# The end of self-attention in a fused transformer layer: first chunk normalized and scored earlier, last products in another order, later chunks ranked one feed-forward step later

## The reference

```python
def reference(x, ctx, mask, Wq, Wk, Wv, Wo, wq, wk, wv, wo, w_router, W1, b1, W2, b2):
    x = x + cross_attention(layernorm(x), ctx, mask)          # ctx: (32, 512, 384)
    x = x + causal_self_attention_with_rope(layernorm(x))     # Wo included in both
    h = layernorm(x)
    scores = h @ w_router                                     # (32, 64)
    top_scores, top_idx = top_k(scores, 32)                   # per sequence, half the tokens
    y = gelu(h[top_idx] @ W1 + b1) @ W2 + b2                  # 512 -> 2048 -> 512
    return x + h.at[top_idx].add(sigmoid(top_scores) * y)
```

## Time and profile before

| | us |
|---|---|
| median of 3 runs | 1379.94 (1377.67 to 1382.29) |
| the profiled execution's own time | 1377.36 |
| its span, first to last instruction | 1374.9 |
| TensorE busy in the span | 1341.6 |
| cross-attention ends, self-attention begins, about | 900 |
| step 14's last TensorE work ends, pe_end begins | 1133.7 |
| the feed-forward begins (first hidden) | 1170.9 |

### The profile page before, as it was taken

How to read it: one execution, slowest core, us unless ns; L and a number is a source line. 1 busy time by engine, 2 the same in 40 slices (tenths; PEclk the granted TensorE clock), 3 DMA queues, 4 the chain that set the end, 5 groups by cost and what they waited for, 6 DMA issues and landing times.

```text
span 1374.9 us, 33152 instructions
## 1 busy us (share of the span) xinstructions
PE 1341.6 (98%) x12984; PEld 1059.8 (77%) x12984; DVE 666.7 (48%) x1688; ACT 730.2 (53%) x1410; POOL 544.3 (40%) x284
## 2 busy tenths in 40 slices
PE   7999999999999999999999999999999998999998
PEld 6877777777777777777777777677888886878686
DVE  4254554554544544544544544455666567732323
ACT  6455655656656656656656656653333345453231
POOL 6442422422522422422432434724444444466342
PEclk9999999999999999999999999999999999999999
DMA  7021111011011010110120112010000002122241
GB/s 254 26 59 34 34 50 32 28 54 32 25 57 32 25 57 26 31 57 25 32 57 25 32 56 93 14 55 2 1 0 0 0 0 93 62 92 92 77 138 61
DMA packets 39324, 66.06 MB, mean 48 GB/s; under 512 B 4208, under 2 KB 8560, under 8 KB 39280
## 3 DMA queue, kind: packets, MB, share of 16 engines
q1 hardware_dynamic: 38848, 64.67, 14.7%
q10 hardware_dynamic: 432, 0.79, 0.2%
HBM read 61.25 MB, written 4.19 MB: 48 GB/s over the span
## 4 chain that ended last, share of the span: by engine, by line
PE 89%; DVE 2%; ACT 2%; issue 1%; POOL 1%; POOLq 0%; DVEq 0%; ACTq 0%
PE psum L204 39%; PE psum L957 9%; PE psum L252 8%; PE psum L1791 6%; PE psum L1762 6%; PE psum L222 5%; PE psum L240 5%; PE psum L261 3%; PE psum L972 3%; PE psum L990 1%; PE psum L1448 1%; PE psum L982 1%; PE psum L1000 1%; PE psum L1773 1%; PE psum L1019 0%
## 5 line engine op out<-in xcount | busy, mean ns | idle before, releaser
L300 ACT ACTIVATE PT<-psum 128x512 f32<-128x512 f32 x256 | 153.2, 598 | 228.4 <-PE psum L252 228.4
L287 ACT ACTIVATE prob<-prob,nmx 128x512 f32<-128x512 f32 x256 | 182.6, 714 | 94.4 <-DVE nmx L342 94.4
L356 DVE COPY V<-psum 128x512 f32<-128x512 f32 x128 | 88.5, 692 | 229.4 <-PE psum L204 229.4
L342 DVE CUSTOM_DVE_ANT_0 prob<-psum,mbias 128x512 f32<-128x512 f32 x256 | 165.4, 684 | 67.1 <-PE psum L222 67.1
L293 ACT ACTIVATE prob<-prob,rinv 128x512 f32<-128x512 f32 x256 | 182.7, 714 | 0.0
L489 POOL TENSOR_SCALAR ctx_a<-ctx_r 128x1536 fp32r<-128x1536 f32 x16 | 65.4, 4090 | 265.3 <-PE psum L204 265.1
L489 POOL TENSOR_SCALAR ctx_b<-ctx_r 128x1536 fp32r<-128x1536 f32 x16 | 65.4, 4090 | 252.3 <-PE psum L204 235.4
L252 PEld LDWEIGHTS psum<-ident,prob 128*128 128x128 f32 x1024 | 127.5, 141 | 34.4 <-issue 1.3
L252 PE MATMUL psum<-ident,prob 128*128 128x128 f32 x1024 | 153.2, 272 | 0.5 <-ACT PT L300 0.4
L204 PE MATMUL psum<-wv_h,ctx_b 128*128 128x512 f32 x384 | 144.4, 417 | 0.0
L204 PE MATMUL psum<-wv_h,ctx_a 128*128 128x512 f32 x384 | 142.2, 412 | 1.2 <-DVE K L356 1.2
(11 more groups left out here) (215 smaller groups left out, 2814.2 us busy)
## 6 DMA issues: line engine op xcount, KB each, us to landing
ctx_r<-in_ctx SPq DMA_DIRECT2D x32, 768.0 KB, 4.6
w_r<-in_L_ffn_W SPq DMA_DIRECT2D x64, 256.0 KB, 2.8
xres<-in_x SPq DMA_DIRECT2D x16, 256.0 KB, 2.6
out<-tok SPq DMA_DIRECT2D x13, 256.0 KB, 3.6
tok<-in_x SPq DMA_DIRECT2D x3, 1024.0 KB, 12.4
mask<-in_mask_BxS_bf SPq DMA_DIRECT2D x32, 64.0 KB, 4.1
tok<-in_x SPq DMA_DIRECT2D x4, 256.0 KB, 3.3
wq_r<-in_L_xattn_Wq SPq DMA_DIRECT2D x4, 256.0 KB, 5.0
```

What stands on the lines that cost most here:

```text
L287: act.activation(prob[:, r, :], prob[:, r, :], ACT.Exp, bias=nmx[:, r:r + 1], scale=-1.0, accum_out=rsum[:, r:r + 1]).then_inc(s_ex, 1)
L300: act.activation(PT[:, r, :, :].rearrange("p k n -> p (k n)"), T_bank, ACT.Copy).then_inc(s_Pt, 1)
L342: dve.tensor_tensor_reduce(prob[:, r, :], S_bank[r], mbias[:, b, :], 1.0, 3.0e38, ALU.add, ALU.min, nmx[:, r:r + 1]).then_inc(s_mx, 1)
L356: dve.tensor_copy(item_place(q, m), KV_bank[m % 2]).then_inc(s_KVe, 1)
```

## The change

No product is added or left out. Parts:

1. **Chunk 0 early.** The deviations of tiles 0 to 7 are made in step 13, those of tiles 8 to 11 in step 14 and dve_end, those of 12 to 15 at the end; before, tiles 0 to 11 in step 14. The four normalizations of chunk 0 move to the end of step 13 (one) and to the start of step 14 (three); chunk 0 takes slot 3 of xn4 and chunk 3 slot 0. Its four dots and the diagonal run in step 14 on VectorE; the statistics of tiles 12 and 13 move from step 14 and the last part of dve_end to its middle. Steps 12 and 13 are written out instead of being turns of the loop.
2. **The last products in another order** (pe_end). V of tile 15 comes after the last transposes of q and k, then the scores of tile 15, the spread of chunk 0, the output projection of tile 13, and only then probabilities and values of tile 14, its output projection (in bank 6), those of tile 15, the spread of chunk 1, both gathers of chunk 0, its transposes, the gathers of chunk 1, the last output projection (in bank 4). VectorE and ScalarE follow that order.
3. **Chunks 2 and 3 later.** The spread of chunk 2 moves from feed-forward step 0 to 1, its gathers from 1 to 2, the spread of chunk 3 behind the second product of step 2; the dots of chunk 2 on VectorE come behind the hid_l of step 0 instead of before the feed-forward. GpSimd's first w_l waits for the one-hots of chunk 1.

```diff
@@ pe3
-            if has(t + 1):
+            if has(t + 1) and not (isinstance(t, int) and t == G - 2):
                 at_least(pe, s3_od, t)
                 project(pe, bank[1], x3_h[:, nxt, :, :], x3_l[:, nxt, :, :], vw_h, vw_l).then_inc(s3_V, 1)
@@ act3
+            if isinstance(t, int) and t == G - 2:
+                act_normalize(act, 0, range(1, CH))
...
-            if isinstance(t, int) and t == G - 2:
-                act_deviations(act, MOST)
+            if isinstance(t, int) and t >= G - 3:
+                act_deviations(act, FIRST if t == G - 3 else MIDDLE)
                 act.activation(warm[:], epsb[:], ACT.Exp)
-                act.wait_ge(s3_K, G)
-                act.wait_ge(s4_nm, 1)
-                act_normalize(act, 0)
...
+            if isinstance(t, int) and t == G - 3:
+                act.wait_ge(s3_wd, 1)
+                act.wait_ge(s4_nm, 1)
+                act_normalize(act, 0, range(1))
@@ last_stats, new: like next_stats, but writes mv3 directly
+        def last_stats(dve, t):
+            dve.wait_ge(s3_x, t + 1)
+            dve.wait_ge(s4_mv, t)
+            dve.bn_stats(st1[:], tok[:, t, :]).then_inc(s4_st, 1)
+            dve.wait_ge(s4_st, t + 1)
+            dve.bn_aggr(mv3[:, t, :], st1[:]).then_inc(s4_mv, 1)
-        MOST, REST = slice(0, G - CH), slice(G - CH, G)
+        FIRST, MIDDLE, REST = slice(0, 2 * CH), slice(2 * CH, 3 * CH), slice(3 * CH, G)
@@ dve3
             if has(t + 1):
+                if isinstance(t, int) and t == G - 2:
+                    dve.wait_ge(s4_c, 16 * 7)
+                    for n in range(CH - 1):
+                        dve_dot(dve, n)
                 dve.wait_ge(s3_K, t + 2)
...
-            if isinstance(t, int) and t == G - 2:
-                dve_deviations(dve, MOST, 0)
...
             if has(t - 1):
                 dve_o(dve, t - 1, 1 - par)
+            if isinstance(t, int) and t == G - 3:
+                dve_deviations(dve, FIRST, 0)
...
-            if has(t - 2):
+            if isinstance(t, int) and t == G - 2:
+                dve_dot(dve, CH - 1)
+                dve_diagonal(dve, 0)
+            elif has(t - 2):
                 next_stats(dve, t - 2)
@@ steps
-            with eng.Fori(1, G // 2 - 1) as h:
+            with eng.Fori(1, G // 2 - 2) as h:
-            for t in range(G - 2, end):
+            for t in range(G - 4, end):
@@
-        BANKS_OF = [(3, 0, 1, 3), (3, 5, 6, 7), (2, 3, 2, 3), (2, 3, 2, 3)]
+        BANKS_OF = [(3, 0, 1, 3), (7, 2, 6, 7), (2, 3, 2, 3), (2, 3, 2, 3)]
@@ pe_end, after the transposes of q and k
+            project(pe, bank[1], x3_h[:, PAR, :, :], x3_l[:, PAR, :, :], vw_h, vw_l).then_inc(s3_V, 1)
+            pe.wait_ge(s3_qa, G)
+            pe.wait_ge(s3_kT, G)
+            pe.wait_ge(s3_ms, LAST)
+            scores(pe).then_inc(s3_S, 1)
+            pe_spread(pe, 0)
+            pe.wait_ge(s3_x, LAST - 2)
+            output_projection(pe, PAR).then_inc(s3_Wo, 1)
             pe.wait_ge(s3_pn, LAST)
-            pe.wait_ge(s3_qa, G)
             pe.wait_ge(s3_v, G)
             for h in range(2):
                 probabilities(pe, 1 - PAR, h).then_inc(s3_PT, 1)
-            pe.wait_ge(s3_kT, G)
-            pe.wait_ge(s3_ms, LAST)
-            scores(pe).then_inc(s3_S, 1)
             pe.wait_ge(s3_pa, 2 * LAST)
             values(pe, 1 - PAR).then_inc(s3_PV, 1)
-            pe.wait_ge(s3_x, LAST - 2)
-            output_projection(pe, PAR).then_inc(s3_Wo, 1)
-            pe.wait_ge(s3_x, LAST - 1)
+            pe.wait_ge(s3_ms, G)
             pe.wait_ge(s3_od, LAST)
-            output_projection(pe, 1 - PAR).then_inc(s3_Wo, 1)
-            pe_spread(pe, 0)
+            output_projection(pe, 1 - PAR, bank[6]).then_inc(s3_Wo, 1)
...
             values(pe, PAR, LAST_BANK).then_inc(s3_PV, 1)
+            pe_spread(pe, 1)
             pe_gather(pe, 0, 0)
             pe_gather(pe, 0, 1)
-            pe_spread(pe, 1)
+            pe_transpose(pe, 0)
             pe.wait_ge(s3_x, LAST)
-            pe.wait_ge(s3_od, G)
-            output_projection(pe, PAR).then_inc(s3_Wo, 1)
             pe_gather(pe, 1, 0)
             pe_gather(pe, 1, 1)
-            pe_transpose(pe, 0)
+            pe.wait_ge(s3_od, G)
+            output_projection(pe, PAR, bank[LAST_BANK]).then_inc(s3_Wo, 1)
             pe_transpose(pe, 1)
@@ act_end: q_T, k_T, v, normalize chunk 1, pT of 14, exp of 15, o_h of 14, three w_h,
@@ then half of chunk 2, pT of 15, o_h of 15, the other half of chunk 2, xs_h ...
@@ dve_end
+            dve_deviations(dve, MIDDLE, 1)
...          (mask and row maximum of tile 15)
+            dve_compare(dve, 0)
+            dve_dot(dve, CH)
+            dve_dot(dve, CH + 1)
+            add(LAST - 2, bank[2])
             dve_o(dve, LAST - 1, 1 - PAR)
...          (row sum and reciprocal of tile 15)
+            last_stats(dve, LAST - 3)
+            last_stats(dve, LAST - 2)
+            dve_dot(dve, CH + 2)
+            dve_dot(dve, CH + 3)
+            dve_diagonal(dve, 1)
             dve_one_hot(dve, 0)
+            add(LAST - 1, bank[6])
             dve_compare(dve, 1)
             dve_one_hot(dve, 1)
+            dve_o(dve, LAST, PAR, LAST_BANK)
@@ gpsimd, feed-forward
+                    if isinstance(n, int) and n == 0:
+                        pool.wait_ge(s4_oh, 2 * CH)
                     if isinstance(n, int) and n == 1:
-                        pool.wait_ge(s4_s, 2 * CH)
                         pool.wait_ge(s3_PV, G)
@@ vector, feed-forward
-                between = {0: lambda: (dve_compare(dve, 2), dve_one_hot(dve, 2)),
-                           1: lambda: (dve_low(dve, 2, 0), dve_low(dve, 2, 1), dve_scores(dve, 3)),
-                           2: lambda: (dve_compare(dve, 3), dve_one_hot(dve, 3)), 3: lambda: (dve_low(dve, 3, 0), dve_low(dve, 3, 1))}
+                between = {0: lambda: dve_scores(dve, 2),
+                           1: lambda: (dve_compare(dve, 2), dve_one_hot(dve, 2), dve_scores(dve, 3)),
+                           2: lambda: (dve_low(dve, 2, 0), dve_low(dve, 2, 1), dve_compare(dve, 3), dve_one_hot(dve, 3)),
+                           3: lambda: (dve_low(dve, 3, 0), dve_low(dve, 3, 1))}
@@ tensor, feed-forward
-                between = {0: lambda: pe_spread(pe, 2), 1: lambda: (pe_gather(pe, 2, 0), pe_gather(pe, 2, 1), pe_transpose(pe, 2)),
-                           2: lambda: pe_spread(pe, 3),
+                between = {0: lambda: (pe.wait_ge(s4_oc, 2), pe.wait_ge(s3_x, G)), 1: lambda: pe_spread(pe, 2),
+                           2: lambda: (pe_gather(pe, 2, 0), pe_gather(pe, 2, 1), pe_transpose(pe, 2)),
                            3: lambda: (pe_gather(pe, 3, 0), pe_gather(pe, 3, 1), pe_transpose(pe, 3))}
...
+                    if isinstance(n, int) and n == 2:
+                        pe_spread(pe, 3)
```

More of the change, by code:

```diff
@@ L966, in pe_x, with output_projection @@
             ins.then_inc(s3_XT, 1)
-        def output_projection(pe, buf):
+        def output_projection(pe, buf, place=bank[2]):
             for n in range(DT):
                 for i, (o, w) in enumerate(((o_h, ow_h), (o_h, ow_l), (o_l, ow_h))):
-                    ins = pe.matmul(bank[2], o[:, buf, n, :, :].rearrange("p b q -> p (b q)"), w[:, n, :],
+                    ins = pe.matmul(place, o[:, buf, n, :, :].rearrange("p b q -> p (b q)"), w[:, n, :],
                                     start=(n == 0 and i == 0), stop=(n == DT - 1 and i == PRODUCTS - 1))
@@ L1410, in dve_low, with act_normalize @@
                               xs_h[:, :, at].bitcast(F32), ALU.subtract).then_inc(s4_gl, 1)
-        def act_normalize(act, c):
-            for t in range(CH):
+        def act_normalize(act, c, tiles=range(CH)):
+            for t in tiles:
                 n = CH * c + t
-                act.activation(xn4[:, c % XN, t, :], tok[:, n, :], ACT.Identity, bias=nmr[:, n:n + 1],
+                act.activation(xn4[:, SLOT_OF[c], t, :], tok[:, n, :], ACT.Identity, bias=nmr[:, n:n + 1],
                                scale=rs3[:, n:n + 1]).then_inc(s4_xn, 1)
@@ L1512, in act_end @@
             copy = lambda o, i: act.activation(o, i, ACT.Copy)
-            act.wait_ge(s3_V, G)
-            act.wait_ge(s3_PV, LAST - 1)
-            copy(v_s[:, PAR, :], bank[1]).then_inc(s3_v, 1)
             act.wait_ge(s3_Tq, G)
@@ L1521, in act_end @@
             copy(k_T[:].rearrange("p n c -> p (n c)"), bank[3]).then_inc(s3_kT, 1)
+            act.wait_ge(s3_V, G)
+            act.wait_ge(s3_PV, LAST - 1)
+            copy(v_s[:, PAR, :], bank[1]).then_inc(s3_v, 1)
+            act_normalize(act, 1)
             for h in range(2):
@@ L1524, in act_end @@
                 copy(p_place(h), bank[h]).then_inc(s3_pa, 1)
-            act.wait_ge(s3_Wo, LAST - 2)
+            act.wait_ge(s3_su, G)
+            last = sm[:, PAR].rearrange("p a b c d -> p (a b c d)")
+            act.activation(last, last, ACT.Exp).then_inc(s3_ex, 1)
             act.wait_ge(s3_PV, LAST)
@@ L1528, in act_end @@
```

(18 more changed lines are left out.)

34 lines of the change are left out of this document (11 added, 23 removed).

## The result

| | before | after |
|---|---|---|
| median of 4 runs, us | 1378.99 (1377.67 to 1382.29) | 1371.74 (1370.06 to 1372.28) |
| the profiled execution's own time | 1377.36 | 1372.28 |
| its span | 1374.9 | 1370.5 |

The ratio is 0.9945, with a 95% interval of 0.9932 to 0.9958: 7.2 us faster. Two later groups of runs of the changed kernel, beside other runs of the kernel before, gave 0.9953 (0.9938 to 0.9968) and 0.9958 (0.9945 to 0.9971). So it is faster by 6 to 7 us; I had said 4.6, in a range from 0.4 to 8.6. The direction, and most of the steps, are right; the size is short by a third. In absolute time the result, 1371.74, lies only 0.4 us above the lower end of my range (1371.3), and 0.95 us of its distance from the forecast 1375.3 comes from the kernel before, whose median came down from 1379.94 to 1378.99 with a fourth run.

The account below looks back on a forecast made before the run. TensorE, busy 98%, bounds the kernel; only seam idle time and low clock can be won. Gaps and clock gone, 7.2 + 3.1, less new gaps 4.6, net -5.7; a new clock fall 1.1 leaves -4.6: 1375.3 us, range 1371.3 to 1379.5.

Parts of the forecast that it names:

- The gap before V and its clock: Before V of tile 15: an earlier o_l of tile 13 removes 1.87 us of gap and 1.66 of low clock.
- The dots in step 14: Three new VectorE dots, 1.9 us in all, fit idle time before the K rotation: cost nothing, at most 0.6.
- The shift in step 13: Shift of tiles 0 to 7 may be held 1.05 us by GpSimd's subtraction, costing TensorE nothing.
- The new waits: In pe_end: +0.78 before tile 14's values, +1.45 before its output projection, +0.5 before the last probabilities.
- the 0.93, 0.49 and 0.36: TensorE gaps before the first hidden and in feed-forward step 0, to go under part 3: -1.8 us.
- hid_l of step 1: Feed-forward: made behind chunk 2's held dots, ready 1176.5; spread and Y(1) want them at 1174.6 and 1175.1: +1.35 us.
- The gaps together: TensorE's waits at the seam of self-attention and feed-forward: 7.2 us gone, 4.6 new.
- the old falls: Low clock behind the 1.87 and 2.20 us gaps, at V of tile 15 and chunk 0's spread: 3.1 us gone.
- The new fall: Clock falls once over tile 14's output projection, behind gaps of 0.78 and 1.45: +1.1 us, bounds 0 and 1.7.
- No clock fall: Rival: the two new gaps are too short or too far apart to lower the clock; net -5.7, chance 0.2.
- The shift is held: Rival: GpSimd holds dve_end's shift, tile 15's chain 1.7 us late, clock surely falls; net -3.5, chance 0.2.
- Slower: Rival: VectorE becomes the bound through GpSimd holds of 13 us; some 8 slower, 1388, chance 0.07.

Follow-up runs that it names:

- the normalizations back: Changed kernel with three normalizations of chunk 0 put back in step 14 between the table load and o_h of tile 13: 1372.46 us, ratio 0.9967 to the kernel before.
- part 1 alone: Kernel before plus only the early chunk 0, with the old order of products and of chunks 2 and 3: 1379.57 us, ratio 1.0011.
- part 3 undone: Changed kernel with chunks 2 and 3 scored and ranked at their old feed-forward steps: 1369.28 us, ratio 0.9944 to the kernel before.
- the second repeat: The unaltered changed kernel run again beside the kernel before, on the same chip as two other experiments: median 1372.79 us of 5 runs, ratio 0.995.

## Why the prediction was right, and where its size was off

All times in this part are on the clock of before (after minus 0.64).

**Part 1, right.** o_l of tile 13 was to be ready at 1133.5: it ran 1132.75 to 1133.43. The gap before V and its clock are gone; with the normalizations back, 1.25 us of gap is back. The dots in step 14 I put at nothing, upper bound 0.6: one took 1.76 us instead of 0.68 beside GpSimd's q_r, and the K rotation was still on time. The shift in step 13 was held as said (below), and nothing waited for it. What I did not say is that part 1 alone would bring nothing.

**Part 2, right in each step.** Forecast and measured: transposes 1133.6 and 1133.59; probabilities of tile 14 at 1141.7 and 1141.57; output projection of tile 14 at 1145.8 and 1145.70; the last probabilities at 1149.35 and 1149.11. The new waits: 0.78 and 0.74, 1.45 and 1.50, 0.5 and 0.41.

**Part 3, the step that failed.** I gave it new waits of 1.35 + 0.5 and counted -1.8 for the 0.93, 0.49 and 0.36 as gone. The new waits measured 0.18 + 0.36 + 0.21 = 0.75; hid_l of step 1 was ready at 1175.3, not 1176.5. And the -1.8 is not part 3's: with part 3 undone these waits stay away as well, all but 0.1 us, since parts 1 and 2 make the dots of chunk 2 early. Part 3 itself costs 1.33 of the seam, where my sum made it nothing (-1.8 + 1.85). Two errors that partly cancel in part 3's own worth: the credit went to the wrong part, and the hold by GpSimd was priced 1.1 too high. In the sum of the whole change only the second one counts.

**The gaps together, the mis-sized term.** Predicted -7.2 + 4.6 = -2.6, measured -3.98; 1.1 of the difference is part 3's waits, the other 0.3 is less than 0.2 each at several places. (Of small gaps in before there are three, 0.35, 0.21 and 0.16, not the four I counted; the sum has the first two.) A second term I put at nothing without saying so: I priced a wait at its idle time alone, and 11 waits that became 8 gave 0.7 us more.

**The clock, right for the old falls.** Predicted -3.1 for the two old falls and +1.1 for a new one, -2.0. The old ones measured -3.0 (1.62 + 1.34). The new fall, which I took as sure, did not come in this execution; it came in one of three executions of the changed kernel, for 0.98. So from -4.6 to the seam's -7.65: 1.4 for gaps, 0.7 for what comes with each wait, 1.1 for the fall that stayed away, less 0.1 for the old falls.

Over all runs the clock's share is nearer to what I said. The mean granted clock was 0.9945 before (22 runs) and 0.9959 after (7 runs beside them). At half speed the loss is the span times one minus the clock, an estimate: 1376.5 x 0.0055 = 7.5 us before, 1370.2 x 0.0041 = 5.7 after, so 1.8 us by the clock (1.7 in the group of the second repeat) against my 2.0. The other 4.4 us of the 6.3 between these mean spans are waits, as are 3.98 + 0.7 of the seam, against my 2.6. That all runs together show more than my 4.6 is therefore due to the waits; that the seam of this one execution shows 7.65 is in part its luck with the clock.

In part 1 alone the loss by the clock is 1377.4 x 0.0079 = 10.9 us, where the kernel before had 6.9 beside it: the 4.0 more are over what the gaps saved (2.3 us by the same sum).

**The rivals.** "No clock fall" (-5.7) was the nearest. "The shift is held" did not come true, but its condition is real and its margin 0.1 us; its price is 0.96, not 2.2, where the clock stays up, as it did in the one profile of it. "Slower" had its holds (0.3 to 2.2 us each, at least six of them), never 10 us together on the path.

Left open: what makes the clock fall in one execution and not in another behind the same gaps; what TensorE waited for in the 2.36 us stop (that it went away with the loads is shown by one execution of each kernel, and in before and after the loads ran beside TensorE, between 1140 and 1148, without a stop); and what part 2 is worth without part 1.

## What to carry to other kernels

When a wait is removed, walk the engine on to the next thing that is late: here a 1.87 us gap only came back as one of 2.29, 3.6 us down the line, until the order of the products was changed too. Put operations with two SBUF inputs on VectorE where GpSimd is idle, and look which of the two is issued first: 0.1 us of order was worth 0.9 us. And test each part of a bundle alone; parts 1 and 2 together gained some 8 us (8.7 by the medians, 1377.95 to 1369.28; 7.7 by the ratio), and the third gave back 1.3 of them unseen. Price a wait at a little more than its idle time: here 0.2 us more each.
